# A windowed multi-level attention and a mixture of experts, one layer in float32: weights laid out by the host, biases carried by the last weight row

## The chip, the cores and the metric

The kernel runs on one core of a Trainium2 chip. The metric is the device time of one execution in microseconds; the time before is the median of three runs. The whole program is written by hand against five engines: TensorE (PE, with its weight loads PEld), VectorE (DVE), ScalarE (ACT), GpSimd (POOL) and SyncE (SP), which here only issues DMAs.

## The reference

x has 2 x 1024 tokens of 128 channels. One layer: x = x + attention(layernorm(x)), then x = x + experts(layernorm(x)).

```python
qkv = x @ W_attn + b_attn                  # 128 -> 384, 16 heads of 8 channels
q, k, v = split(qkv, 3)
# level 0: each query sees the 64 keys up to its own; levels 1 to 4: the 8 mean-pooled keys
# of the previous block of 64, 128, 256, 512 tokens (pools of 8, 16, 32, 64 tokens)
mn = min over levels of max(A_level)       # the shift of the exponentials
out = sum over levels of scale * exp(A - mn) / esum @ (v, pooled v)
x = x + out @ W_proj + b_proj
...
gate = softmax(x @ Wg.T); keep the best 2 of 8, divide by their sum
for e in range(8):                         # all experts are computed, and weighted
    a, b = split(x @ W1[e].T + b1[e], 2)   # 128 -> 2 x 256
    out += ((a * sigmoid(b)) @ Wo.T + bo) * comb[..., e]
```

## The kernel before

A function schedule() writes one list of steps, and every engine runs through that one list and does its own part of each step. So each engine's order is fixed by hand, and the engines are tied by semaphores. An instruction that waits holds up all that stands behind it on its engine.

Precision: a product of two float32 tensors is made of three products of fast-format (fp32r) parts, high x high, high x low, low x high (`split3`, L1045 to L1047). For that each operand is split: a copy writes the high part, a subtraction the low part. A few products are plain float32, which the profile counts as two instructions each.

Attention. Batch b goes in four units of 4 heads, units 0 to 3 for batch 0 and 4 to 7 for batch 1. Before a batch's units: `stat` and `apply` (layer norm, xnorm), `xT` (four PE transposes, xT_hi copied by ScalarE, xT_lo by VectorE), `pool` (pooled means of xT, 128 x 512: xpool_hi, xpool_lo), `qk` (query and key products, q, k times 512 tokens each), `kp` (pooled keys), `v` and `pv` (values and pooled values, four groups each). In a unit, tiles of `score` are followed three tiles later by their `out` products (L1198, L1199), with ScalarE's exponential and VectorE's `mask` (L978) in between. `guard` (VectorE maxima of pooled scores, L954 to L957), `shift` and `shiftT` give the shift row of the next unit. SP moves the parts of q, k and pooled k of a unit's heads into the tiles qst, kst and pks by DMA; `heads` (`head_columns`, L410, or L408 on VectorE) spreads pks into pkm, one column set per head.

Where biases are handled before:
- q, k: `bias` makes columns of the q and k bias (two products of one row, L1061) and of b1 (a transpose, L1062); VectorE copies both (L886, L887). ScalarE and VectorE add the column while they split q and k (L685, L928).
- pooled k: VectorE adds the column and multiplies with a mask of real blocks (L934), then copies the high part (L936) and subtracts (L937).
- v, pooled v: in each of the four groups of a step a fourth product of 2 rows adds the bias, split into two rows (L1087, L1093). `constants` (L830 to L835) makes these rows on VectorE. There are two v steps and one pv step in each batch.
- w1: a channel of ones is put in the last column of xnorm (L722), the last column of w1 is taken from the others by GpSimd (L622), and b1 put in its place (L623). Layer-normed channels sum to zero, so that one of them can be given up.

Weights: `weights` permutes and scales W_attn on VectorE (L819 to L823) and splits it (L824, L825). W1 comes as it is, (expert, 512, 128), in tiles of 256 KB, through a ring of STAGES = 4 buffers; the steps `w1` stand at score tiles 1, 1, 2, 3, 4, 6, 7 and 9 of the last unit: SP's load, GpSimd's subtraction (L622, L623), four PE transposes (L1122), ScalarE's copy of the high part (L701) and VectorE's subtraction (L1001). `w2` does the same for Wo and Wg (L1126, L1127). One of three general banks of PSUM is used by each step of the set GENERAL in turn.

Experts (from about 222 us): for each of 16 tiles of 128 tokens and each of 8 experts three products of 512 columns, a sigmoid, a product with the gate on VectorE (L1028), an addition on GpSimd (L654), then two transposes and the output product.

The first instructions of GpSimd are memsets: of qmk (128 x 4096), vwin and vaug (128 x 2048, and four narrow ones, L607), for each of two buffers.

## Time and profile before

| what | us |
|---|---|
| median of 3 runs | 335.55 |
| all three runs | 335.55, 331.0, 336.18 |
| the profiled execution, its time | 336.18 |
| its span, first to last instruction | 336.2 |
| TensorE busy | 305.9 (91%) |
| VectorE busy | 226.8 (67%) |
| ScalarE busy | 178.1 (53%) |
| GpSimd busy | 142.3 (42%) |
| mean granted TensorE clock | 0.929 |

The profile shows one execution. Busy is the time in which an engine has an instruction in flight, so for TensorE, whose instructions overlap, a busy stretch need not be a fast one. The clock that was granted to TensorE is given as a share of 2.4 GHz, so 0.5 is 1.2 GHz. HBM read is 4.21 MB and written 1.05 MB over the span.

### The profile page before, as it was taken

The page shows a single profiled execution, that of the slowest core. Times are in us where ns is not written, and L with a number is a line of the kernel's source. Part 1 is how long each engine was busy: PE and PEld are TensorE (multiplying, and loading weights), DVE is VectorE, ACT ScalarE, POOL GpSimd, SP SyncE. Part 2 cuts the span into 40 slices and gives each one's busy share as a digit, 9 for nine tenths or more (in the row PEclk, how much of TensorE's full clock was granted, in tenths as well). Part 3 has the DMA queues.
Part 4 walks back from the last instruction along what each step waited for, and adds up shares of the span by engine and source line. Part 5 has one row for each costly group of instructions (what it writes and reads, how often), then busy time and mean ns, then how long its engine had stood idle before and what let it go on. Part 6 is the DMA issues. An engine that isn't in the chain of part 4 may idle for free.

```text
span 336.2 us, 6934 instructions
## 1 busy us (share of the span) xinstructions
PE 305.9 (91%) x2384; PEld 260.7 (78%) x2384; DVE 226.8 (67%) x660; ACT 178.1 (53%) x366; POOL 142.3 (42%) x232
## 2 busy tenths in 40 slices
PE   0268699899999999999999999999999999999995
PEld 0246589788988989887989899886888867888884
DVE  6997408987585550285666655947786798777773
ACT  1513166557546842654576654574548655555552
POOL 3990011330012100010050665208778847888882
PEclk9997555999999997589999979999999999999999
DMA  7005405252304500033526013000000000000000
GB/s 225 27 1 121 104 18 117 57 118 59 96 11 94 127 18 10 1 89 101 118 64 179 11 50 108 4 10 8 8 10 18 11 0 16 11 16 8 11 17 17
DMA packets 15881, 17.51 MB, mean 52 GB/s; under 512 B 2235, under 2 KB 12646, under 8 KB 15846
## 3 DMA queue, kind: packets, MB, share of 16 engines
q1 hardware_dynamic: 15648, 16.85, 19.4%
q8 instruction: 19, 0.31, 0.4%
q10 hardware_dynamic: 198, 0.22, 0.3%
q14 instruction: 16, 0.13, 0.1%
HBM read 4.21 MB, written 1.05 MB: 16 GB/s over the span
## 4 chain that ended last, share of the span: by engine, by line
PE 76%; DVE 14%; issue 4%; ACT 3%; POOL 1%; DMA 1%; ACTq 0%; DVEq 0%
PE bank L1198 16%; PE bank L1045 12%; PE bank L1047 11%; PE bank L1046 11%; PE bank L1172 5%; PE bank L1179 4%; PE bank L1199 4%; PE bank L1100 2%; PE bank L1159 2%; PE bank L1087 2%; DVE xnorm L802 2%; DVE lmax L954 2%; PE bank L1122 2%; DVE work L978 1%; DMA xres<-L_attn_x 1%
## 5 line engine op out<-in xcount | busy, mean ns | idle before, releaser
L654 POOL TENSOR_TENSOR work<-work 128x256 f32<-128x256 f32 x110 | 80.9, 739 | 33.6 <-DVE work L1028 21.0
L1198 PE MATMUL bank<-work,vaug 128*64 128x64 f32 x1024 | 84.1, 231 | 0.3 <-issue 0.3
L1198 PEld LDWEIGHTS bank<-work,vaug 128*64 128x64 f32 x1024 | 72.8, 143 | 8.9 <-issue 1.2
L1028 DVE SCALAR_TENSOR_TENSOR work<-bank,comb,work 128x256 f32<-128x256 f32 x128 | 59.1, 480 | 25.7 <-ACT work L759 24.4
L759 ACT ACTIVATE work<-bank 128x256 f32<-128x256 f32 x128 | 48.4, 385 | 44.7 <-PE bank L1047 44.5
L978 DVE TENSOR_TENSOR work<-work,const 128x512 f32<-128x512 f32 x64 | 46.2, 734 | 18.0 <-ACT work L737 17.4
L586 POOL COPY vaug<-vwin 128x64 f32<-128x64 f32 x64 | 16.1, 298 | 94.8 <-ACT vwin L697 48.0
L737 ACT ACTIVATE work<-bank 128x512 f32<-128x512 f32 x64 | 37.5, 594 | 27.2 <-PE bank L1179 26.8
L1199 PE MATMUL bank<-work,vpool 128*64 128x64 f32 x256 | 36.9, 227 | 0.0
L562 POOL TENSOR_TENSOR rstd<-veps,nhalf 128x4 f32<-128x4 f32 x8 | 11.5, 1432 | 49.6 <-DVE veps L794 49.5
L1179 PE MATMUL bank<-qmk,kst 98*128 98x256 f32 x128 | 31.0, 328 | 0.0
L1045 PE MATMUL bank<-qmk,xT_hi 128*128 128x512 f32 x64 | 27.4, 428 | 0.1
L1045 PE MATMUL bank<-qmk,kst 128*128 128x512 f32 x64 | 26.5, 414 | 0.0
L1199 PEld LDWEIGHTS bank<-work,vpool 128*64 128x64 f32 x256 | 26.2, 143 | 0.0
L1047 PE MATMUL bank<-qmk,xT_lo 128*128 128x512 f32 x64 | 25.3, 395 | 0.0
L1046 PE MATMUL bank<-arena,xT_hi 128*128 128x512 f32 x64 | 25.3, 395 | 0.0
L1047 PE MATMUL bank<-qmk,kst 128*128 128x512 f32 x64 | 25.1, 392 | 0.0
L1046 PE MATMUL bank<-arena,kst 128*128 128x512 f32 x64 | 25.0, 391 | 0.0
L410 ACT ACTIVATE pkm<-pks,const 96x512 fp32r<-96x512 f32 x30 | 20.8, 712 | 5.5 <-DMA pks<-kpool_hi 5.5
L1179 PEld LDWEIGHTS bank<-qmk,kst 98*128 98x128 f32 x128 | 21.6, 209 | 2.4 <-issue 0.8
L954 DVE TENSOR_REDUCE lmax<-bank 128x12 f32<-128x96 f32 x64 | 13.5, 252 | 13.1 <-PE bank L1100 12.6
L1172 PE MATMUL bank<-qst,pkm 104*128 104x64 f32 x128 | 20.0, 309 | 0.0
(194 smaller groups left out, 534.6 us busy)
## 6 DMA issues: line engine op xcount, KB each, us to landing
qst<-arena SPq DMA_DIRECT2D x24, 128.0 KB, 2.3
kst<-arena SPq DMA_DIRECT2D x24, 128.0 KB, 2.3
qmk<-qst SPq DMA_DIRECT2D x32, 96.0 KB
pks<-kpool_hi SPq DMA_DIRECT2D x16, 64.0 KB, 2.0
xnorm<-L_ffn_W SPq DMA_DIRECT2D x4, 256.0 KB, 2.9
out<-yout SPq DMA_DIRECT2D x16, 64.0 KB, 1.5
xres<-L_attn_x SPq DMA_DIRECT2D x2, 256.0 KB, 4.2
xres<-L_attn_x SPq DMA_DIRECT2D x1, 512.0 KB, 7.3
```

The source lines that it names most:

```text
L654: gp.tensor_tensor(gacc[t % 2][:, :], gacc[t % 2][:, :], gtmp[(adds - 1) % TMP_RING][:, :], ALU.add).then_inc(acc_done, 1)
L737: act.activation(prob[lo % P_RING][:, :, :, :], bank[sc % SCORE_BANKS][:, :].rearrange("p (c j q) -> p c j q", c=2, j=GH), ACT.Exp).then_i ...
L759: act.activation(sig[hn % SIG_RING][:, :], bank[hn % HID_BANKS][:, HID:2 * HID], ACT.Sigmoid).then_inc(sig_done, 1)
L978: dve.tensor_tensor(prob[lo % P_RING][:, :, :, :].rearrange("p c j q -> p (c j) q"), prob[lo % P_RING][:, :, :, :].rearrange("p c j q -> p ...
L1028: dve.scalar_tensor_tensor(dst[:, :], bank[hn % HID_BANKS][:, 0:HID], comb[:, t, e:e + 1], sig[hn % SIG_RING][:, :], ALU.mult, ALU.mult).t ...
L1045: pe.matmul(out, lhs[0], rhs[0], start=start, stop=False)
L1046: pe.matmul(out, lhs[0], rhs[1], start=False, stop=False)
L1047: return pe.matmul(out, lhs[1], rhs[0], start=False, stop=stop)
L1172: ins = pe.matmul(out[:, k * WIN:(k + 1) * WIN], pkm[s][0:SR + 2 * GH, c, :, :].rearrange("p j k -> p (j k)"), qst[s][0:SR + 2 * GH, c * W ...
L1179: ins = pe.matmul(out[:, k * 256:(k + 1) * 256], kst[s][0:SR + 2, c * WIN:c * WIN + P], qmk[s][0:SR + 2, :, c * WIN:(c + 1) * WIN], start= ...
L1198: pe.matmul(o, vaug[hu % 2][:, c % 8, j, :], prob[lo % P_RING][:, i, j, :], start=(j == 0), stop=False)
L1199: ins = pe.matmul(o, vpool[:, c, u % NG, :], probp[u % 2][:, c, :], start=False, stop=True)
```

## The change

The host now hands over weights that are already laid out. W_attn comes with q and k columns permuted, W1 transposed to (128, 8, 512), Wo and Wg transposed. For wqkv, w1 and wg it comes in two planes: in plane 0 the last row is the bias, in plane 1 every row holds a copy of the last row of the weights, its own last row being zero. Plane 0 minus plane 1 is then the weight with its last row taken from all others and the bias in its place. The last channel of xnorm is one, for the first layer norm too, and GpSimd writes these ones once (`ones_ready`). So the sums over 128 rows bring the bias with them:

- gone: the step `bias` (three TensorE instructions, two VectorE copies), the four copies and scalings of `weights` and bias_perm, the step `constants`, the 24 bias products, the 32 transposes of w1, the three of wo and wg, the four ScalarE copies of ones, GpSimd's column copies of w1 and its two steps on wg, and three small loads on ScalarE's queue;
- pooled k: padded blocks of xpool are zero in all rows, so no mask. ScalarE makes the high part from PSUM, VectorE the low part;
- q is scaled while it is split (0.35 or 1 as a number, no bias column);
- w1: GpSimd subtracts plane 1 from plane 0 (128 x 512), ScalarE copies the high part from SBUF, VectorE subtracts from SBUF. Tiles are of 512 KB, the ring has 3 buffers, two of them new. The first two loads wait for nothing new, the third for the second x2T step, and each later one for VectorE's subtraction of the tile three before (`w1_ready`);
- wqkv is one load of 384 KB; the constants shrink from 504 KB to 182 KB.

```diff
-GENERAL = {"bias", "xT", "qk", "kp", "v", "pv", "guard", "shiftT", "spread", "proj", "w1", "w2", "x2T", "gatelog", "hidT", "y"}
+GENERAL = {"xT", "qk", "kp", "v", "pv", "guard", "shiftT", "spread", "proj", "x2T", "gatelog", "hidT", "y"}
-ACT_FIRST = {"xT", "qk", "w1", "x2T"}
+ACT_FIRST = {"xT", "qk", "kp", "x2T"}
...
-    s += [("qk", 0, 0, 0), ("qk", 0, 0, 1), ("kp", 0), ("constants",), ("qk", 0, 1, 0), ("qk", 0, 1, 1)]
+    s += [("qk", 0, 0, 0), ("qk", 0, 0, 1), ("kp", 0), ("qk", 0, 1, 0), ("qk", 0, 1, 1)]
...
-STAGES = 4
+STAGES = 3
...
+    def paired(w, bias):
+        rows = np.array(w, np.float32)
+        rows[C - 1] = bias
+        last = np.array(np.broadcast_to(w[C - 1], w.shape), np.float32)
+        last[C - 1] = 0.0
+        return rows, last
...
             def load_w1(n):
-                sp.dma_start(w1_stage[n % STAGES], w1_d[n].rearrange("(t p) c -> p t c", p=P)).then_inc(w1_in[n % STAGES], 16)
+                sp.dma_start(w1_stage[n % STAGES][:, :, :], w1_d[:, n]).then_inc(w1_in[n % STAGES], 16)
...
                 if u + 2 == UNITS:
-                    wait_gen_full(sp, ("pv", 1))
-                    wait_gen_full(sp, ("x2T", 0, 0))
                     for i in range(STAGES - 1):
                         load_w1(i)
             wait_gen_full(sp, ("x2T", 0, 1))
             load_w1(STAGES - 1)
             for n in range(STAGES, E):
-                wait_gen_done(sp, ("w1", n - STAGES))
+                sp.wait_ge(w1_ready, n - STAGES + 1)
                 load_w1(n)
...
+            gp.memset(xnorm[:, :, C - 1:C], 1.0).then_inc(ones_ready, 1)
             blank_keys(0)
             rstd_of(0)
...
-            def fix_w1(n):
+            def whole_w1(n):
                 st = w1_stage[n % STAGES]
-                wait_gen_done(gp, ("bias",))
                 gp.wait_ge(w1_in[n % STAGES], 16 * (n // STAGES + 1))
-                then(gp.tensor_tensor(st[:, :, 0:C - 1], st[:, :, 0:C - 1], st[:, :, C - 1:C].broadcast_to([P, 4, C - 1]), ALU.subtract))
-                gp.tensor_copy(st[:, :, C - 1:C], b1_col[:, 4 * n:4 * n + 4].unsqueeze(2)).then_inc(w1_fixed, 1)
+                gp.tensor_tensor(st[:, 0, :], st[:, 0, :], st[:, 1, :], ALU.subtract).then_inc(w1_whole, 1)
...
-                elif step == ("gatelog", 0, 1):
-                    for n in range(STAGES):
-                        fix_w1(n)
-                elif step[0] == "w1" and step[1] >= STAGES:
-                    fix_w1(step[1])
+                elif step[0] == "w1":
+                    whole_w1(step[1])
...
+                elif kind == "kp":
+                    b = step[1]
+                    wait_gen_full(act, step)
+                    if b:
+                        act.wait_ge(pks_in, 48 * NG)
+                    act.activation(kpool_hi[:, :], gen_bank(step)[:, :], ACT.Copy).then_inc(gen_hi, 1)
...
                 elif kind == "w1":
                     n = step[1]
-                    wait_gen_full(act, step)
-                    act.activation(w1T_hi[:, n, :], gen_bank(step)[:, :], ACT.Copy).then_inc(gen_hi, 1)
+                    act.wait_ge(w1_whole, n + 1)
+                    act.activation(w1T_hi[:, n, :], w1_stage[n % STAGES][:, 0, :], ACT.Copy).then_inc(w1_high, 1)
...
-                    ins = dve.tensor_scalar(xnorm[:, t, :], xres[:, t, :], mv[:, o + i, 0:1], rstd[:, o + i:o + i + 1], ALU.subtract, ALU.mult)
+                    ins = dve.tensor_scalar(xnorm[:, t, 0:C - 1], xres[:, t, 0:C - 1], mv[:, o + i, 0:1], rstd[:, o + i:o + i + 1], ALU.subtract, ALU.mult)
...
-                dve.wait_ge(wattn_in, 64)
-                dve.tensor_scalar(by_row(bias_perm[:, 0:C]), by_d(bias_row[:, 0:C]), QSCALE, None, ALU.mult)
-                dve.tensor_copy(by_row(bias_perm[:, C:2 * C]), by_d(bias_row[:, C:2 * C]))
-                dve.tensor_scalar(by_row(wqkv[:, 0:C]), by_d(wattn[:, 0:C]), QSCALE, None, ALU.mult)
-                dve.tensor_copy(by_row(wqkv[:, C:2 * C]), by_d(wattn[:, C:2 * C]))
-                then(dve.tensor_copy(wqkv[:, 2 * C:3 * C], wattn[:, 2 * C:3 * C]))
+                dve.wait_ge(wqkv_in, 16)
+                then(dve.tensor_tensor(wqkv[:, 0, :], wqkv[:, 0, :], wqkv[:, 1, :], ALU.subtract))
...
-                    then(dve.scalar_tensor_tensor(kpool[:, :], bk[:, :], bias_col[:, 1:2], const[:, C_PADMASK:C_PADMASK + NB * LK],
-                                                  ALU.add, ALU.mult))
-                    then(dve.tensor_copy(kpool_hi[:, :], kpool[:, :]))
-                    dve.tensor_tensor(kpool_lo[:, :], kpool[:, :], kpool_hi[:, :].bitcast(F32), ALU.subtract).then_inc(gen_dve, 1)
+                    dve.tensor_tensor(kpool_lo[:, :], bk[:, :], kpool_hi[:, :].bitcast(F32), ALU.subtract).then_inc(gen_dve, 1)
...
-                    pe.wait_ge(cst_ready, 1)
                     pe.wait_ge(xt_ready, 2 * b + n + 1)
...
-                        split3(out, (xT_hi[:, rows], xT_lo[:, rows]), wv, stop=False)
-                        ins = pe.matmul(out, rows2[:, NB * LK:NB * LK + P], bv2[:, :], start=False, stop=True)
+                        ins = split3(out, (xT_hi[:, rows], xT_lo[:, rows]), wv)
...
-                    for i in range(4):
-                        ins = pe.transpose(bk[:, i * P:(i + 1) * P], w1_stage[step[1] % STAGES][:, i, :], ident)
```

What moves on the engines is shown at three places, before first and then now; the names are tiles, written <- read.

VectorE at the start, from the end of the layer norm of batch 0 on. Before (attT holds the weights, denom the bias):

```order
L819 TENSOR_SCALAR attT<-denom 1x128
L820 COPY attT<-denom 1x128
L821 TENSOR_SCALAR attT<-attT 128x128
L822 COPY attT<-attT 128x128
L823 COPY attT<-attT 128x128
L824 CAST wqkv_hi<-attT 128x384
L825 TENSOR_TENSOR wqkv_lo<-attT,wqkv_hi 128x384
L905 TENSOR_TENSOR xT_lo<-bank,xT_hi 128x512
L906 TENSOR_REDUCE pool_sum<-bank 128x64
L905 TENSOR_TENSOR xT_lo<-bank,xT_hi 128x512
L906 TENSOR_REDUCE pool_sum<-bank 128x64
L886 COPY bias_col<-bank 128x2
```

Now, at the same place, with planes and result both in attT:

```order
L807 TENSOR_TENSOR attT<-attT 128x384
L808 CAST wqkv_hi<-attT 128x384
L809 TENSOR_TENSOR wqkv_lo<-attT,wqkv_hi 128x384
L873 TENSOR_TENSOR xT_lo<-bank,xT_hi 128x512
L874 TENSOR_REDUCE pool_sum<-bank 128x64
L873 TENSOR_TENSOR xT_lo<-bank,xT_hi 128x512
L874 TENSOR_REDUCE pool_sum<-bank 128x64
L881 TENSOR_TENSOR pool_sum<-pool_sum 128x64
```

Five small steps in front of the cast became one wider subtraction, and the copies behind the pooled sums are gone.

TensorE in the first v step of batch 1, behind the third unit's out products. Before:

```order
L1045 MATMUL bank<-wqkv_hi,xT_hi 128x128
L1046 MATMUL bank<-wqkv_lo,xT_hi 128x128
L1047 MATMUL bank<-wqkv_hi,xT_lo 128x128
L1087 MATMUL bank<-bv,rows 128x128
L1045 MATMUL bank<-wqkv_hi,xT_hi 128x128
L1046 MATMUL bank<-wqkv_lo,xT_hi 128x128
L1047 MATMUL bank<-wqkv_hi,xT_lo 128x128
L1087 MATMUL bank<-bv,rows 128x128
```

Now:

```order
L1012 MATMUL bank<-wqkv_hi,xT_hi 128x128
L1013 MATMUL bank<-wqkv_lo,xT_hi 128x128
L1014 MATMUL bank<-wqkv_hi,xT_lo 128x128
L1012 MATMUL bank<-wqkv_hi,xT_hi 128x128
L1013 MATMUL bank<-wqkv_lo,xT_hi 128x128
L1014 MATMUL bank<-wqkv_hi,xT_lo 128x128
```

The fourth product of each group is gone; the groups follow each other directly.

SP's queue of loads at the last unit of attention, where xpool, kpool and xnorm served as buffers of w1. Before:

```order
L437 DMA xpool<-L_ffn_W 128x4x128 [waits gen_full]
L437 DMA kpool<-L_ffn_W 128x4x128
L437 DMA xnorm<-L_ffn_W 128x4x128
L434 DMA qmk<-nshiftT 2x32x128 [waits gen_dve]
L434 DMA qst<-nshiftT 8x8x128
L437 DMA xnorm<-L_ffn_W 128x4x128 [waits gen_full]
L437 DMA xpool<-L_ffn_W 128x4x128 [waits gen_dve]
L437 DMA kpool<-L_ffn_W 128x4x128 [waits gen_dve]
L437 DMA xnorm<-L_ffn_W 128x4x128 [waits gen_dve] x2
```

Now, with w_stage for the two new buffers:

```order
L441 DMA w_stage<-w 128x1024 x2
L438 DMA qmk<-nshiftT 2x32x128 [waits gen_dve]
L438 DMA qst<-nshiftT 8x8x128
L441 DMA xnorm<-w 128x1024 [waits gen_full]
L441 DMA w_stage<-w 128x1024 [waits w1_ready] x2
L441 DMA xnorm<-w 128x1024 [waits w1_ready]
L441 DMA w_stage<-w 128x1024 [waits w1_ready] x2
```

The first loads lost their wait, one fewer is made ahead, and the later ones wait for VectorE's subtraction of w1 (`w1_ready`).

## Rows read from the trace of the kernel before

**Rows 1.** Busy time by stretch: stretch, length, PE, PEld, DVE, ACT, POOL, PEclk, DMA, GB/s

```profile
3.00:4.00 1.00, 0.00 (x0) 0.00 (x0) 0.62 (x2) 0.75 (x1) 0.00 (x0) 1.00 1.11 338
30.20:57.50 27.30, 24.43 (x100) 20.90 (x100) 12.64 (x50) 13.40 (x26) 2.49 (x9) 0.50 0.33 80
125.80:129.20 3.40, 3.40 (x33) 3.28 (x31) 0.22 (x1) 2.07 (x4) 0.00 (x0) 0.51 0.07 19
132.60:146.30 13.70, 13.70 (x70) 12.42 (x69) 5.10 (x15) 8.97 (x19) 1.48 (x8) 0.50 0.02 4
206.00:222.00 16.00, 16.00 (x209) 14.71 (x207) 12.76 (x52) 7.87 (x15) 5.38 (x10) 1.00 0.07 20
222.00:336.00 114.00, 109.90 (x544) 88.94 (x542) 82.86 (x227) 62.07 (x162) 83.73 (x116) 1.00 0.04 11
```

**Rows 2.** Timeline of the start, VectorE and GpSimd: start us, us, engine, line, operation

```profile
14.61 1.09 POOL L607 MEMSET vaug<- 128x64 f32 x4
...
15.40 0.51 DVE L824 CAST wqkv_hi<-attT 128x384 fp32r<-128x384 f32 x1
...
15.94 0.56 DVE L825 TENSOR_TENSOR wqkv_lo<-attT,wqkv_hi 128x384 fp32r<-128x384 f32 x1
...
20.68 1.80 POOL L605 MEMSET vaug<- 128x2048 f32 x1
20.71 2.06 DVE L922 CAST xpool_hi<-xpool 128x512 fp32r<-128x512 f32 x1
...
22.55 0.54 POOL L607 MEMSET vaug<- 128x64 f32 x4
```

**Rows 3.** Timeline, pooled keys, key splits and head columns of units 0 and 1

```profile
25.30 0.75 DVE L934 SCALAR_TENSOR_TENSOR kpool<-bank,bias_col,const 128x512 f32<-128x512 f32 x1 [0.48 <-PE bank L1047]
...
26.08 0.43 DVE L936 CAST kpool_hi<-kpool 128x512 fp32r<-128x512 f32 x1
...
26.54 0.69 DVE L937 TENSOR_TENSOR kpool_lo<-kpool,kpool_hi 128x512 fp32r<-128x512 f32 x1
...
28.76 1.39 DVE L928 SCALAR_TENSOR_TENSOR arena<-bank,bias_col,arena 128x512 fp32r<-128x512 f32 x2
...
30.45 1.33 ACT L410 ACTIVATE pkm<-pks,const 96x512 fp32r<-96x512 f32 x2 [2.34 <-DMA pks<-kpool_hi]
...
45.04 2.55 ACT L410 ACTIVATE pkm<-pks,const 96x512 fp32r<-96x512 f32 x4
```

**Rows 4.** Timeline of TensorE, v products around a bias product, at both clocks

```profile
122.04 0.27 PE L1046 MATMUL bank<-wqkv_lo,xT_hi 128*128 128x128 f32 x1
122.15 0.27 PE L1047 MATMUL bank<-wqkv_hi,xT_lo 128*128 128x128 f32 x1
...
122.61 0.33 PE L1045 MATMUL bank<-wqkv_hi,xT_hi 128*128 128x128 f32 x1
...
138.49 0.41 PE L1047 MATMUL bank<-wqkv_hi,xT_lo 128*128 128x128 f32 x1
...
139.24 0.48 PE L1045 MATMUL bank<-wqkv_hi,xT_hi 128*128 128x128 f32 x1
```

**Rows 5.** Timeline of the last unit of attention, w1 beside it

```profile
200.09 0.37 SPq L437 DMA_DIRECT2D xpool<-L_ffn_W  x1
...
201.61 0.66 PE L1122 MATMUL bank<-const,xnorm 128*128 128x128 f32 x4
...
202.03 0.48 PE L1179 MATMUL bank<-qmk,kst 98*128 98x256 f32 x2
...
203.14 1.03 POOL L622 TENSOR_TENSOR xpool<-xpool 128x508 f32<-128x508 f32 x1 [4.28 <-DMA xpool<-L_ffn_W]
...
203.55 1.18 DVE L978 TENSOR_TENSOR work<-work,const 128x512 f32<-128x512 f32 x1
...
205.13 0.60 ACT L701 ACTIVATE qmk<-bank 128x512 fp32r<-128x512 f32 x1 [1.74 <-PE bank L1122]
```

**Rows 6.** DMA issues of w1 tiles: KB each, median us from issue to landing

```profile
xnorm<-L_ffn_W SPq DMA_DIRECT2D x4, 256.0 KB, 2.9
```

More of the change, by code:

```diff
@@ L136, in schedule @@
 def schedule():
-    s = [("stat", 0, 0), ("stat", 0, 1), ("apply", 0, 0), ("apply", 0, 1), ("weights",), ("xT", 0, 0), ("xT", 0, 1), ("bias",), ("pool", 0)]
-    s += [("qk", 0, 0, 0), ("qk", 0, 0, 1), ("kp", 0), ("constants",), ("qk", 0, 1, 0), ("qk", 0, 1, 1)]
+    s = [("stat", 0, 0), ("stat", 0, 1), ("apply", 0, 0), ("apply", 0, 1), ("weights",), ("xT", 0, 0), ("xT", 0, 1), ("pool", 0)]
+    s += [("qk", 0, 0, 0), ("qk", 0, 0, 1), ("kp", 0), ("qk", 0, 1, 0), ("qk", 0, 1, 1)]
     s += [*[("heads", 0, j) for j in range(GH)], ("weight columns",), ("v", 0, 0), *[("guard", 0, m) for m in range(4)], ("shift", 0), ("shiftT", 0)]
@@ L163, in schedule @@
         5: {5: [("stat2", 0, 0)], 8: [("apply2", 0, 0)]},
-        6: {0: [("x2T", 0, 0)], 4: [("stat2", 0, 1)], 7: [("apply2", 0, 1)], 8: [("w2",), ("x2T", 0, 1)]},
+        6: {0: [("x2T", 0, 0)], 4: [("stat2", 0, 1)], 7: [("apply2", 0, 1)], 8: [("gate weights",), ("x2T", 0, 1)]},
         7: {0: [("gatelog", 0, 0)], 3: [("gatelog", 0, 1)], 4: [("gatelog", 0, 2)], 5: [("gatelog", 0, 3)],
@@ L342, in build @@
         zero_ready = sem("zero_ready")
+        ones_ready = sem("ones_ready")
         heads_ready = sem("heads_ready")
@@ L1057, in _ @@
                         wait_gen_done(pe, GEN[n - GEN_BANKS])
-                if kind == "bias":
-                    pe.wait_ge(wqkv_ready, 1)
-                    for t in range(2):
-                        ins = pe.matmul(bk[:, t:t + 1], bias_perm[0:1, t * C:(t + 1) * C], const[0:1, C_ONES:C_ONES + 1], start=True, stop=True)
-                    ins = pe.transpose(bk[:, P:P + 4 * E], b1_rows, ident[0:4 * E, 0:4 * E])
-                elif kind == "xT":
+                if kind == "xT":
                     _, b, n = step
```

168 lines of the change are left out of this document (60 added, 108 removed).

## The prediction

> **What bounds the kernel now.** I read the table of stretches first. From 222 us on, the expert phase, TensorE is busy 109.90 of 114.00 us at the full clock [rows 1]; the change edits nothing that repeats there, so a third of the span is fixed. In the attention before it TensorE is the late engine too, but its clock falls to half for three stretches: 30.2 to 57.5, 125.8 to 129.2 and 132.6 to 146.3, 44 us in all [rows 1]. In the first of them TensorE counts as busy 24.43 of 27.30 us while VectorE does 12.64; what it runs at the half clock is then paid double. Then the timeline of the start: up to 30 us VectorE carries the path and TensorE waits for it (xnorm, weights, xT_lo, pooling). Last the stretch from 206 to 222 us, where w1 is prepared beside the last unit of attention: TensorE 16.00 of 16.00 busy, VectorE 12.76 [rows 1]. So work taken from VectorE pays before 30 us, work taken from TensorE pays in 35 to 50 and 120 to 150 us, and at 206 to 222 us it pays only until VectorE is late.
>
> **The profiled execution.** It is the run of 336.18 us, its span 336.2; nothing lies around it. The median of the three runs is 335.55, the fastest 331.0. I sum against 336.2 and read the result against 335.55.
>
> **Start, VectorE up to the keys.** The four permuting copies (L820 to L823) stand beside GpSimd's four small memsets at 14.61, and the cast behind them begins at 15.40 [rows 2]: 0.8 us, 0.2 each. They give way to one subtraction of 128x384, for which I take the 0.56 of L825, the same size [rows 2]: 0.2 saved. The two copies of bias columns (L886, L887) go, which wait for nothing by then; by the permuting copies they are worth 0.4, but they are narrower, and I take 0.2. Then comes a race. The cast of xpool_hi took 2.06 us, its twin of kpool_hi 0.43 [rows 2, 3]: it was issued at 20.71, 0.03 us behind a GpSimd memset of 1.80 us, and ended when that ended. 0.4 us earlier it would be in front. But the four small memsets took 1.09 us beside the permuting copies and 0.54 without them [rows 2], so GpSimd comes 0.5 us earlier too and again stands in front by about 0.1. I take the cast as still blocked and ending with the memset, 0.75 us earlier in all; the other end is 2.2 us, if it slips ahead. The new subtraction reads two SBUF tensors and the memsets read none. The Trainium skill (SBUF — State Buffer, Who interferes with whom) says that a copy or cast takes the port pair shared with GpSimd while a subtraction of two SBUF tensors meets only GpSimd instructions that read; the trace agrees for the copies (1.09 against 0.54), and shows no such subtraction.
> Pooled keys: behind the products three VectorE steps ran from 25.30 to 27.23 [rows 3]. Now ScalarE copies (0.60, as L701 in rows 5) and VectorE subtracts (0.69): about 1.4, so 0.55 saved. Their DMAs, issued by SP behind it, and the first head columns (ScalarE, 30.45 [rows 3]) come 1.3 us earlier. The split of the v bias, six small steps between 27.23 and 28.76 [rows 3], leaves VectorE; TensorE's v products waited for it, and ScalarE's v copies, which free the bank of the third guard, waited for them. I put another 1.3 us on this, 2.6 in all when the first shift row is transposed. Against it: wqkv comes as 384 KB instead of 192 beside the first x tile; at 338 GB/s [rows 1] half of the extra 192 KB is 0.3 us, taken off.
>
> **The 24 bias products on TensorE.** From the product before one to the product behind it: 0.46 us at the full clock (122.15 to 122.61), 0.75 at half (138.49 to 139.24) [rows 4]. Without it that step lies between the 0.11 inside a group (122.04 to 122.15 [rows 4]), which would make the bias product worth 0.35, and half of the 0.46, which makes it 0.23; I take 0.27, and at the half clock 0.48 (up to 0.53). Of six groups of four, the first ran while others waited; the second and the pooled one of batch 0 lie in the slow stretch, 1.9 us each. From the second group on, ScalarE waits for its DMA of pooled keys instead, so I count 0.7 of it until the head columns of unit 1 (45.04 [rows 3]) and 1.8 for the pooled one. The start gives 2.6 + 0.7 + 1.8 - 0.3 = **4.8 us**, bounds 2.5 and 7. Batch 1: two groups at full clock, 1.1 each, one at half, 1.9: **4.1 us**, TensorE having no idle time there.
>
> **The clock in batch 1.** Both falls, at 125.8 and 132.6 [rows 1], come right behind a group of v or pooled v products, the first of which is the group of 122.04 [rows 4]. In such a group four products of 2 rows stand among twelve full ones; without them it is 1.1 us shorter, and the dense out products beside it move up. If the two falls vanish, 3.4 + 1.2 us of out products run at twice the speed (2.3 us), and score, v and key products up to 146.3 gain 1 to 2 us more, ScalarE's head and pool copies then being late (8.97 us busy of 13.70 [rows 1]). Bounds 0 and 4.3; I take **3.0**.
>
> **The end of attention.** Eight groups of four transposes of w1 go, 0.42 us each (201.61 to 202.03 [rows 5]): 3.4; three products of wo and wg, 0.4 by the same row. But w1 now comes in three stages of 512 KB where it had four of 256 KB. The reload is triggered as before, when the first stage is free (SP, 200.09 [rows 5]), but brings tile 3, where it brought tile 4. Landing: 2.9 us for 256 KB [rows 6] and 0.8 for the rest at 338 GB/s, an estimate of 3.7. Then GpSimd subtracts 128x512 with two full inputs, 1.0 to 1.4 (1.03 [rows 5]), and ScalarE copies at 200.09 + 3.7 + 1.3 = 205.1. It copied tile 3 at 205.13 [rows 5]. So the time freed in front of it is absorbed by this wait: behind it in ScalarE's queue stand the exponentials of the next score tiles, which TensorE needs three tiles later, so it is not held, but VectorE's queue (subtraction, mask, gates) starts no earlier. From 206 on VectorE has 3.2 us idle [rows 1], which bounds the gain; half a microsecond of it lies behind its last gate step, and eight subtractions that now read two SBUF tensors meet GpSimd's reading (a mask took 1.18 beside GpSimd's of 203.14 [rows 5], where 128x512 is else worth the 0.69 of L937 [rows 3]), some 0.5 lost. **2.3 us**, and 0.6 for gate and wo; 0 to 4.4. The same section of the Trainium skill has that contention as its rule, two SBUF inputs against GpSimd reads; the mask agrees.
> ScalarE loses four column copies, VectorE's xnorm a column, both hidden by TensorE: nothing. The rest is the same.
> Sum: 4.8 + 4.1 + 3.0 + 2.9 = 14.8, so 336.2 - 14.8 = **321.4 us**.
>
> **Rivals.** A: the clock falls in batch 1 as before. For it: score tiles and v products remain sparse around 134 us. 324.4, and with the end worth less, up to 327. B: the cast wins its race, the keys come 1.4 us earlier and the rest goes by the upper bounds: 313 to 317. C: the w1 ring becomes the path. Two rounds of reload must fit between 200.09 [rows 5] and about 219 us; each is the landing plus 1.3 on GpSimd, 0.6 on ScalarE and 0.7 on VectorE. It decides when a landing takes over some 6 us, (18.9 - 5.2) / 2 = 6.8 with none of the queues in between busy; at 9 us two rounds cost 5 more and the gain at the end turns into a loss: 326 to 329. D, slower: the clock stays at half after the start. TensorE now has longer holes around 30 us, waiting for keys and shifts, and the attention behind them at half clock pays 0.5 us for each us so spent. It must outlast the present 57.5 us by 24 us to eat the 11.8 us of the other terms, by 38 to be 2% slower: about 343 to 350. Against it: the out products that stand at 57.5 come earlier and are unchanged. E: all is hidden, at 331 to 335: the start would have to wait for a DMA that no row shows as late.
>
> **Chances.** Forecast (318 to 324) 0.45, A 0.24, B 0.13, C 0.11, D 0.02, E 0.05. Eight in ten lie between 315 and 328.5. Within 2% of 335.55, about what a measurement of this kernel can tell from no change, means over 328.8: the top of C and all of E, 0.1.
>
> **What would show it.** The first head columns near 29.2 us, those of unit 1 near 41.7 (30.45 and 45.04 [rows 3]); xpool_hi again about as long as a memset or 0.4 us (B). No half clock at 125 to 132 less the 5 us gained (A: it is there). ScalarE waiting for GpSimd before the copy of w1 tile 3, one wait of 2 to 3 us; waits before tiles 5 to 7 as well would be C. First expert product some 14.8 us before the 222 us of [rows 1]. The forecast is wrong if the start gives under 3 us, or if half-clock time grows.

## The result, and the profile after

The changed kernel takes 323.06 us (median of four runs, 322.82 to 323.71), the kernel before 335.87 (four runs, 331.0 to 336.33): a ratio of 0.970, 95% interval 0.962 to 0.978. The forecast was 321.4. The changed kernel ran twice more, on two chips, at 323.58 and 323.30 us. Nearly all its executions lie between 322.6 and 324.6; those of the kernel before, over all chips, between 330.7 and 339.4. The ratios here and below leave out executions that lie more than 1.5% above the fastest of their kernel, so they differ a little from the quotients of the medians.

First a correction of the base. The profiled execution of the changed kernel took 322.97 us and spans 320.8. Executions of the kernel before that were listed with both numbers took 1.8 us more than their span, 337.92 for 336.1 in one. So the one with the span of 336.2 took about 338.0 and was not the run of 336.18: it stood 2 us above the median. Span against span the change gives 15.4 us, where the sum was 14.8. Median against median it gives 12.8.

The profile's page of the changed kernel, busy time by engine and the granted clock in 40 slices:

```profile
span 320.8 us, 6751 instructions
PE 285.0 (89%) x2320; PEld 244.2 (76%) x2320; DVE 221.3 (69%) x643; ACT 178.1 (56%) x364; POOL 142.6 (44%) x223
PEclk9999557999999999699999979999999999999999
```

Busy time by stretch, to be held against [rows 1]; the first three are the stretches at half clock, the fourth is the last unit of attention, the last the experts:

```profile
31.80:52.20 20.40, 15.96 (x80) 14.96 (x80) 10.36 (x46) 11.05 (x23) 2.49 (x9) 0.51 0.33 82
127.20:134.20 7.00, 5.96 (x34) 5.26 (x34) 3.83 (x12) 5.40 (x10) 1.99 (x8) 0.52 0.16 36
185.40:188.90 3.50, 3.50 (x28) 3.09 (x27) 2.03 (x4) 3.02 (x6) 0.00 (x0) 0.56 0.56 156
181.22:206.40 25.18, 23.73 (x279) 21.76 (x277) 17.97 (x60) 13.79 (x25) 10.69 (x10) 0.93 0.37 124
206.40:320.80 114.40, 110.10 (x544) 88.94 (x542) 82.97 (x227) 62.00 (x160) 83.83 (x116) 1.00 0.04 11
```

The experts are as they were (114.4 against 114.0 us, PE 110.10 against 109.90). The half clock at the start lasts 20.4 us where it lasted 27.3 (23.9 in e10, the changed kernel once more). Of the two falls around 130 us one is left, 7.0 us in place of 17.1. The third row, at 185 us, is not new: the kernel before has the same short fall in its last unit, which [rows 1] and the prediction's "three stretches" leave out. It is in both kernels and explains none of the gain; in the kernel before it is

```profile
197.40:200.80 3.40, 3.40 (x21) 3.18 (x21) 1.27 (x2) 2.38 (x5) 1.37 (x3) 0.50 0.02 5
```

The timeline of the start, to be held against [rows 2, 3]:

```profile
12.93 1.81 POOL L608 MEMSET vaug<- 128x2048 f32 x1
13.16 1.66 DVE L807 TENSOR_TENSOR attT<-attT 128x384 f32<-128x384 f32 x1
...
16.62 3.52 POOL L598 MEMSET qmk<- 128x4096 f32 x1
...
19.13 1.05 DVE L885 TENSOR_SCALAR xpool<-pool_sum 128x120 f32<-128x120 f32 x4
...
20.19 1.81 POOL L608 MEMSET vaug<- 128x2048 f32 x1
...
20.22 2.06 DVE L890 CAST xpool_hi<-xpool 128x512 fp32r<-128x512 f32 x1
...
24.81 0.60 ACT L681 ACTIVATE kpool_hi<-bank 128x512 fp32r<-128x512 f32 x1 [4.52 <-PE bank L1014]
...
29.44 1.33 ACT L414 ACTIVATE pkm<-pks,const 96x512 fp32r<-96x512 f32 x2 [1.48 <-DMA pks<-kpool_hi]
```

The cast was issued half a microsecond earlier, and so was the memset: it stands 0.03 us behind it again and takes 2.06 us again. These rows show that it was no race. The last of the four scalings of xpool in front of the cast waits for the memset of qmk (it ends at 20.14, the scalings at 20.18), and GpSimd's next memset begins right behind that end. In the kernel before the two ends are 20.63 and 20.67, in e5 below the lag is 0.03 us again (20.47 and 20.49). So here GpSimd's memsets set the pace in both kernels, and 0.4 us less work on VectorE could not have put the cast in front. The new subtraction ends with a memset too: 1.66 us in place of the 0.56 taken for it. The step ahead of it was held as long, so this cost nothing: the cast of wqkv_hi begins 0.53 us earlier (14.87 for 15.40). The first head columns start at 29.44 us (29.2 was forecast), those of unit 1 at 41.31 (41.7).

The timeline of the last unit, w1 tile 3 on its way through SP, GpSimd, ScalarE and VectorE, to be held against [rows 5]:

```profile
185.87 0.93 SPq L441 DMA_DIRECT2D w_stage<-w  x2
...
189.86 2.50 POOL L624 TENSOR_TENSOR w_stage<-w_stage 128x512 f32<-128x512 f32 x2 [5.09 <-DMA w_stage<-w]
...
191.16 0.63 ACT L696 ACTIVATE qmk<-w_stage 128x512 fp32r<-128x512 f32 x1 [2.65 <-POOL w_stage L624]
...
191.82 1.09 DVE L968 TENSOR_TENSOR arena<-w_stage,qmk 128x512 fp32r<-128x512 f32 x1 [2.14 <-ACT qmk L696]
```

From the load at 185.87 to GpSimd's first subtraction pass 3.99 us (3.7 had been estimated for the landing), ScalarE waits 2.65 us for it and VectorE 2.14 us for ScalarE. That is the wait that the prediction put there. Before, TensorE was busy for all 27.03 us of this unit; now for 23.73 of 25.18.

Where the time went is best seen at fixed points of the program. The table has when each begins, in us of the span, for every kernel of this study (the experiments follow below):

| kernel | first out product | v, batch 1 | unit 4 | unit 5 | unit 7 | experts | span |
|---|---|---|---|---|---|---|---|
| before | 55.31 | 121.87 | 133.83 | 159.24 | 195.01 | 222.04 | 336.2 |
| changed | 49.99 | 116.57 | 123.44 | 145.53 | 181.22 | 206.40 | 320.8 |
| e0_after_again | 49.95 | 116.51 | 123.38 | 145.46 | 181.14 | 206.14 | 320.5 |
| e10_after_third | 50.04 | 116.62 | 123.48 | 145.63 | 181.30 | 206.43 | 320.8 |
| e1_products_back | 53.05 | 119.63 | 132.18 | 157.69 | 193.36 | 219.92 | 334.3 |
| e2_products_second_half | 50.21 | 116.80 | 127.20 | 152.62 | 188.31 | 213.25 | 327.6 |
| e3_before_without_products | 51.30 | 117.87 | 124.73 | 146.84 | 182.60 | 209.54 | 323.7 |
| e9_full_row_products | 50.80 | 117.39 | 125.14 | 153.10 | 189.18 | 214.76 | 329.1 |
| e11_before_full_rows | 52.12 | 118.69 | 126.45 | 148.56 | 184.32 | 211.33 | 325.5 |
| e4_four_stages | 50.04 | 116.60 | 123.47 | 146.07 | 181.74 | 205.12 | 319.5 |
| e12_two_stages | 50.04 | 116.62 | 123.49 | 145.59 | 181.27 | 214.81 | 329.3 |
| e5_memset_in_eighths | 48.84 | 115.40 | 122.26 | 144.88 | 180.55 | 206.40 | 320.7 |
| e7_all_memsets_in_eighths | 44.35 | 110.92 | 117.79 | 139.88 | 175.56 | 200.49 | 314.8 |
| e8_stages_and_eighths | 44.18 | 110.77 | 117.64 | 139.74 | 175.42 | 199.28 | 313.6 |

So the 15.4 us come from the start (5.3 at the first out product), from 121 to 159 us (another 8.4), and from the last unit (1.85); nothing from anywhere else, and the experts take 0.2 us more. From the first out product to v of batch 1 every kernel takes 66.6 us.

### The profile page after: what moved, and what is told of

Read it like the earlier page. It is cut to its first block, busy times and chain, and to the rows that moved or that the text cites. A ratio compares the mean times of both kernels' runs of the same rounds, so it can differ in the third digit from the quotient of the medians.

```text
span 320.8 us, 6751 instructions
## 1 busy us (share of the span) xinstructions
PE 285.0 (89%) x2320; PEld 244.2 (76%) x2320; DVE 221.3 (69%) x643; ACT 178.1 (56%) x364; POOL 142.6 (44%) x223
## 3 DMA queue, kind: packets, MB, share of 16 engines
HBM read 6.16 MB, written 1.05 MB: 22 GB/s over the span
## 4 chain that ended last, share of the span: by engine, by line
PE 65%; DVE 19%; ACT 5%; DMA 4%; issue 4%; POOL 2%; SPq 1%; DVEq 0%; ACTq 0%
PE bank L1148 14%; PE bank L1012 11%; PE bank L1014 10%; PE bank L1013 10%; PE bank L1122 4%; PE bank L1129 4%; DVE work L940 3%; PE bank L1149 3%; PE bank L1060 3%; PE bank L1109 2%; DVE xnorm L796 2%; DVE lmax L916 2%; ACT vpool L400 1%; DMA xres<-x 1%; PE bank L1068 1%
## 5 line engine op out<-in xcount | busy, mean ns | idle before, releaser
L1148 PEld LDWEIGHTS bank<-work,vaug 128*64 128x64 f32 x1024 | 72.1, 142 | 10.3 <-DVE work L940 1.8
L588 POOL COPY vaug<-vwin 128x64 f32<-128x64 f32 x64 | 18.5, 336 | 79.1 <-PE bank L1149 43.4
L1122 PE MATMUL bank<-qst,pkm 104*128 104x64 f32 x128 | 18.1, 291 | 1.4 <-DMA qst<-nshiftT 1.4
```

What stands on the lines that cost most here:

```text
L1122: ins = pe.matmul(out[:, k * WIN:(k + 1) * WIN], pkm[s][0:SR + 2 * GH, c, :, :].rearrange("p j k -> p (j k)"), qst[s][0:SR + 2 * GH, c * W ...
L1148: pe.matmul(o, vaug[hu % 2][:, c % 8, j, :], prob[lo % P_RING][:, i, j, :], start=(j == 0), stop=False)
```

## Experiments on the bias products

All are run beside the kernel before, on the same chip; the changed kernel is repeated with e1, e2 and e3 (as e0) and with e8 and e9 (as e10), the other runs were made without it on their chips. The profiled executions of e1 and e9 were longer than the median of their kernel (336.12 against 334.68, 330.9 against 325.51), that of e7 shorter (316.97 against 319.33); what is said of their totals goes by the medians.

**e0_after_again**, no edit.

> The changed kernel unedited, on the chip of the runs sent with it, as their base. Expected: 322.5 to 324 us, half clock again in three stretches (about 20, 7 and 3.5 us long).

323.58 us (322.62 to 326.07), half clock from about 31, 126.5 and 184.5 us.

**e1_products_back**, and the same for pooled v; zrow holds zeros.

```diff
-                        ins = split3(out, (xT_hi[:, rows], xT_lo[:, rows]), wv)
+                        ins = split3(out, (xT_hi[:, rows], xT_lo[:, rows]), wv, stop=False)
+                        ins = pe.matmul(out, zrow[:, :], wqkv_hi[0:2, 2 * C:3 * C], start=False, stop=True)
```

> The changed kernel with a fourth product of 2 rows (all zeros) put back behind each of the 24 groups of three of v and pooled v; it adds nothing to the sums. Theory (the prediction's): the products cost 2.5 us in batch 0 (0.7 and 1.8) and 4.1 in batch 1, and with them the clock falls at 125.8 and 132.6 come back, 3.0: 332 to 333 us in all, with a half-clock stretch right behind the first v group of batch 1. Rival 1, the products alone: the falls stay away, 329 to 330. Rival 2, the products were hidden in the kernel before: under 326.

334.68 us (329.04 to 338.02; ratio to the kernel before 0.990, 0.982 to 0.998), over the 332 to 333 that were expected. By the medians 11.1 us of the gain are gone again by this edit alone; the host's layout and all that left VectorE, ScalarE and GpSimd is still in it. But its ten executions differ by 9 us, and the granted clock says why. Span times 2 times (1 - mean clock) gives the time at half clock: 31 us in the two shortest (spans of 327.2 and 327.4, mean clock 0.953), as many as in two of e0 (320.5 and 322.1, both 0.952); 46 us in one of 331.3 (0.931), 55 in the profiled one of 334.3 (0.918). So the products cost 5 to 7 us with no more half clock than in the changed kernel, and what the longer ones lost beyond that goes with more half clock. (Where the mean clock is above 0.96 this sum can't be used: the record can lack a stretch, see e3.) Its timeline of TensorE in the first v group of batch 1, and its busy time in two stretches at half clock:

```profile
121.37 0.28 PE L1016 MATMUL bank<-wqkv_hi,xT_lo 128*128 128x128 f32 x1
121.58 0.32 PE L1052 MATMUL bank<-wqkv_hi,zrow 2*128 2x128 f32 x1
121.83 0.33 PE L1014 MATMUL bank<-wqkv_hi,xT_hi 128*128 128x128 f32 x1
```

```profile
122.60:126.40 3.80, 3.80 (x38) 3.59 (x38) 0.88 (x2) 2.95 (x5) 0.00 (x0) 0.55 0.06 17
129.60:146.90 17.30, 17.30 (x91) 15.66 (x92) 7.30 (x20) 9.13 (x20) 1.47 (x8) 0.51 0.12 27
```

From the product before that of 2 rows to the one behind it are again 0.46 us, as in [rows 4], and both falls of the clock are back in this execution, the first right behind the v group, which runs from 119.63 to about 122.6.

**e2_products_second_half**: the same edit, for batch 1 alone.

```diff
-                        ins = split3(out, (xT_hi[:, rows], xT_lo[:, rows]), wv)
+                        ins = split3(out, (xT_hi[:, rows], xT_lo[:, rows]), wv, stop=not b)
+                        if b:
+                            ins = pe.matmul(out, zrow[:, :], wqkv_hi[0:2, 2 * C:3 * C], start=False, stop=True)
```

> As the run with all products back, but the product of 2 zero rows stands only behind the 12 groups of batch 1. Theory: 4.1 us of products and up to 3.0 of clock, 329 to 330.5 us; the start up to the first out product as in the changed kernel (50.0 us). Rival, the clock falls of the kernel before were tied to what batch 0 did before them, not to the products beside them: 327 us, no half clock at the v group of batch 1.

329.60 us (328.80 to 330.86), 6.0 over the changed kernel. At unit 5 it is 7.2 us behind e0 and 0.3 of that stood there at the first out product. One long stretch at half clock, by the busy time in it:

```profile
125.80:140.00 14.20, 14.20 (x79) 12.92 (x77) 5.43 (x17) 9.09 (x19) 1.48 (x8) 0.52 0.02 6
```

In e0 it is 6.8 us long there. The rival's 327 us is out. But it was right that no fall comes with the v group in this run (it ended near 120); the one fall there is comes half a microsecond behind the pooled v group (its last product begins at 125.11). In the changed kernel the fall at 127 comes 5 us behind that group, so "right behind the group" does not hold as a rule.

**e3_before_without_products**: the kernel before, without L1087 and L1093 (the v bias is left out).

```diff
-                        split3(out, (xT_hi[:, rows], xT_lo[:, rows]), wv, stop=False)
-                        ins = pe.matmul(out, rows2[:, NB * LK:NB * LK + P], bv2[:, :], start=False, stop=True)
+                        ins = split3(out, (xT_hi[:, rows], xT_lo[:, rows]), wv)
```

> The kernel before without its 24 products of 2 rows (the v bias is left out of the result), all else as it was. Theory: 2.5 us of batch 0, 4.1 of batch 1 and 3.0 of clock are the products' share, so 9.6 us under the kernel before, near 326 us, and no half clock at 125.8 and 132.6 less the gain ahead of them. Rival, the falls are owed to the score tiles around them, and the products to nothing but their own time: 329 to 330, with half clock near 130 for about 17 us as before.

325.60 us (324.23 to 325.73; ratio 0.973, 0.963 to 0.984): four fifths of the whole gain with none of the change's other parts (10.3 of 12.3 us by the medians of this chip, 12.5 of 15.4 by spans). The time is as expected; that no half clock would be left at this place is not: the stretch around 130 us is 7.2 us long, as in the changed kernel:

```profile
28.80:56.00 27.20, 22.42 (x110) 20.72 (x111) 16.36 (x60) 14.57 (x28) 2.49 (x9) 1.00 0.42 101
127.70:134.90 7.20, 6.21 (x38) 5.50 (x38) 3.58 (x12) 6.17 (x12) 1.99 (x8) 0.53 0.12 29
```

The first of these rows nearly misled me: the clock record says 1.00 from 28.8 to 56 us, as if the fall at the start were gone. The timeline of the same stretch says otherwise:

```profile
30.41 0.41 PE L1046 MATMUL bank<-wqkv_lo,xT_hi 128*128 128x128 f32 x1
30.62 0.41 PE L1047 MATMUL bank<-wqkv_hi,xT_lo 128*128 128x128 f32 x1
```

The step is 0.21 us, twice the 0.11 of the full clock [rows 4], and the steps stay that long until about 56 us. The record was missing, not the half clock.

**e9_full_row_products**: as e1, with

```diff
-        zrow = sb("zrow", [2, P], F32R)
+        zrow = sb("zrow", [P, P], F32R)
-                        ins = pe.matmul(out, zrow[:, :], wqkv_hi[0:2, 2 * C:3 * C], start=False, stop=True)
+                        ins = pe.matmul(out, zrow[:, :], wqkv_hi[:, 2 * C:3 * C], start=False, stop=True)
```

> As the run with the 24 products back, but each takes 128 rows of zeros in place of 2. It has the same columns and the same count. Theory (what the products of 2 rows cost is their own shape: the step over one took 0.35 us more at full clock where a product of 128 rows takes 0.11): each costs 0.11 us, 0.21 at half clock, 4 us in all, and the clock goes as in the changed kernel: 325 to 328 us. Rival: any fourth product costs what those of 2 rows did and brings the longer half clock: 333 to 335.

325.51 us (324.57 to 330.90; ratio 0.976, 0.969 to 0.984): 2.2 us over the changed kernel on its chip (e10), where e1, with the same number of products and columns, was 11.1 over it on its own (e0). The timeline of TensorE, first v group of batch 1:

```profile
118.56 0.28 PE L1016 MATMUL bank<-wqkv_hi,xT_lo 128*128 128x128 f32 x1
118.67 0.28 PE L1052 MATMUL bank<-wqkv_hi,zrow 128*128 128x128 f32 x1
118.78 0.27 PE L1014 MATMUL bank<-wqkv_hi,xT_hi 128*128 128x128 f32 x1
```

0.11 us for the product of 128 rows. A group of three takes 0.33 us, with a product of 128 zero rows 0.44, with one of 2 rows 0.74 (121.09 to 121.83 in e1). So a product of 2 rows costs 0.40 us at full clock and one of 128 costs 0.11. In the profiled execution, the longest at 330.9 us, there is no half clock from 121 to 136 us but some from 140 to 154: the clock can still fall, and the medians have to say how often that matters.

The Trainium skill (TensorEngine Tiling (Array Packing), Key Properties) says that TensorE is drained when the tiling mode changes. These rows fit that: in e1 the steps are 0.21 us ahead of the product of 2 rows, 0.25 behind it and 0.16 behind the next, where 0.11 is usual. The change from products of 128 columns to the out products of 64 shows it too: 0.20 us from 121.93 to 122.13 in the changed kernel, where 0.11 is usual. That the product of 2 rows ran in another mode, no row says; from the last product of 104 rows to the next of 128 rows it is 0.11 us (163.64 to 163.75 in the changed kernel).

**e11_before_full_rows**: the same on the kernel before; `constants` fills all rows of rows2 and the first two of bv2.

```diff
-        rows2 = sb("rows2", [2, NB * LK + P], F32R)
-        bv2 = sb("bv2", [2, C], F32R)
+        rows2 = sb("rows2", [P, NB * LK + P], F32R)
+        bv2 = sb("bv2", [P, C], F32R)
...
+            dve.memset(bv2[:, :].bitcast(F32), 0.0)
```

> The kernel before, with its weights, transposes and constants as they were; its 24 bias products now have 128 rows, of which 126 are zeros, and give the same sums. Theory (two rows are what was dear): the run without these products was 12.5 us shorter in its profile and 24 products of 128 rows cost 2.7 us at full clock and up to 1.2 more at half, so 326 to 329 us where the kernel before takes 332 to 336 on the same chip. Rival: in the kernel before, the products' place counts and not their rows, and it stays within 2 us of the kernel before.

327.30 us (325.95 to 327.84) against 336.42 on that chip (ratio 0.972, 0.969 to 0.974): 9.1 us less. By spans it is 10.7 of the change's 15.4, seven tenths, had by padding an operand with zeros. (Ratios of different chips are not compared here, since the kernel before had medians from 332.0 to 336.4.) The time at half clock around 130 us is down to

```profile
132.60:136.00 3.40, 3.40 (x25) 3.18 (x26) 2.66 (x9) 3.06 (x6) 1.31 (x5) 0.50 0.08 19
```

## Experiments on the ring of w1 and on the start

**e4_four_stages**: a fourth buffer, where the pooled keys lie (kpool_hi and kpool_lo become the halves of kpool_parts); for that the first loads wait until the last pooled keys have been moved (`pks_in`).

```diff
-STAGES = 3
+STAGES = 4
-            ... sb("w1_stage2", [P, 2, 2 * HID]), xnorm[:, 0:TT, :].rearrange("p (n t) c -> p n (t c)", n=2)]
+            ... sb("w1_stage2", [P, 2, 2 * HID]), kpool_parts[:, :, :].bitcast(F32), xnorm[:, 0:TT, :].rearrange("p (n t) c -> p n (t c)", n=2)]
```

> The changed kernel with four stages for w1 instead of three (the fourth lies where the pooled keys were), so that tile 3 is loaded before the last unit. Theory (the reload absorbs part of what the transposes gave back): ScalarE's 2.65 us wait at 191.16 and VectorE's 2.14 us wait behind it go, the first expert product comes 1 to 2 us earlier, 321.3 to 322.3 us. Rival: VectorE has as many instructions before the first expert product as it has time, and waits somewhere else: under 0.5 us, 323.

321.72 us (321.34 to 323.67; ratio 0.968, 0.951 to 0.985, a wide interval since the kernel before spread on that chip); 1.3 to 1.9 us under the changed kernel's three medians. The last unit takes 23.38 us in place of 25.18. Part of this can be the clock: this profile has no half clock in the last unit, the changed kernel's has 3.4 us of it. e7 and e8 below, both with a short fall there, give 24.93 us with three buffers and 23.86 with four, 1.1 us. ScalarE, timeline of the last unit:

```profile
188.92 0.62 ACT L697 ACTIVATE qmk<-xnorm 128x512 fp32r<-128x512 f32 x1
...
191.57 0.63 ACT L697 ACTIVATE qmk<-w_stage 128x512 fp32r<-128x512 f32 x1 [1.55 <-POOL w_stage L625]
```

Tile 3 no longer waits; tile 4 now does, 1.55 us where tile 3 waited 2.65.

**e12_two_stages**; `w1_stage2` leaves the list of buffers.

```diff
-STAGES = 3
+STAGES = 2
```

> The changed kernel with two stages for w1 in place of three. Theory (the ring is on the path in the last unit, and each reload of a stage takes the DMA and three engines, 5 to 7 us): only two tiles are ready ahead and six are loaded behind one another in pairs, three rounds in place of two, so the last unit gets 3 to 6 us longer, 326 to 329 us. Rival: the last unit is held by VectorE's own work, and the ring costs under 1 us, 324.

330.88 us (330.34 to 331.46; ratio 0.983, 0.980 to 0.985). The sign is right and the size is not: 7.3 to 7.8 us over the changed kernel's three medians, more than the upper end of 6. Timeline of ScalarE in the last unit:

```profile
191.05 0.63 ACT L696 ACTIVATE qmk<-w_stage 128x512 fp32r<-128x512 f32 x1 [3.77 <-POOL w_stage L624]
...
197.90 0.63 ACT L696 ACTIVATE qmk<-w_stage 128x512 fp32r<-128x512 f32 x1 [4.43 <-POOL w_stage L624]
...
210.47 0.63 ACT L696 ACTIVATE qmk<-xnorm 128x512 fp32r<-128x512 f32 x1 [3.45 <-POOL xnorm L624]
```

Besides the three waits, the granted clock in this profile is at half from 195 to 205.5 and from 212 to 215.5 us, which neither theory had; how much of the loss it took was not separated. The last unit takes 33.5, 25.2 and 23.4 us with two, three and four stages.

**e5_memset_in_eighths**

```diff
-                then(gp.memset(vaug[i][:, :, :, :], 0.0))
+                for k in range(NB // 2):
+                    ins = gp.memset(vaug[i][:, k, :, :], 0.0)
+                then(ins)
```

> The changed kernel with GpSimd's two memsets of vaug (1.81 us each) written as eight of an eighth. Theory: the cast of xpool_hi is held by the one memset it meets, so it takes at most 0.7 us in place of 2.06, and pooled keys, first head columns and all behind them come 1.3 to 1.4 us earlier: 321.7 us. Rival: GpSimd keeps the cast waiting through all eight in a row, 2 us again, and the time stays at 323.

323.06 us (321.95 to 325.00). The cast that was meant is freed, and the time doesn't follow. The cast of xpool_hi, which meets the first of the eight pieces (they run from 20.47 to 22.83), and TensorE late in the last unit:

```profile
20.49 0.56 DVE L892 CAST xpool_hi<-xpool 128x512 fp32r<-128x512 f32 x1
```

```profile
200.94 0.68 PE L1150 MATMUL bank<-work,vaug 128*64 128x64 f32 x8 [2.10 <-DVE work L942]
```

The first out product comes 1.15 us earlier than in the changed kernel, unit 7 still 0.7, the experts not at all. Half a microsecond is lost between unit 4 and unit 5, beside the stretch at half clock, as in e4, where no instruction up to there is another than in the changed kernel. The rest goes in the last unit, at w1: GpSimd waits 5.13 and then another 0.98 us for the two tiles loaded together (one of these loads took 5.5 us to land, in the changed kernel none there over 4.8), ScalarE 2.63 and 1.40 us for GpSimd, TensorE up to 2.10 us for VectorE.

The pieces also did harm once, in an earlier place. The cast of wqkv_hi, 0.54 us in the changed kernel, was issued behind the third of the first eight pieces and ended 0.2 us behind the last of them (15.04):

```profile
12.88 2.16 POOL L609 MEMSET vaug<- 128x256 f32 x8
...
13.69 1.57 DVE L810 CAST wqkv_hi<-attT 128x384 fp32r<-128x384 f32 x1
```

That is what the rival had, VectorE kept waiting through a row of pieces, at a cast that the expectation did not look at.

**e7_all_memsets_in_eighths**: as e5, and

```diff
-                gp.memset(qmk[i][:, :, :].bitcast(F32), 0.0).then_inc(zero_ready, 1)
+                for j in range(8):
+                    ins = gp.memset(qmk[i][:, j // 2, (j % 2) * T // 2:(j % 2 + 1) * T // 2].bitcast(F32), 0.0)
+                ins.then_inc(zero_ready, 1)
```

> As the run with the vaug memsets in eighths, and the two memsets of qmk (3.51 us each) in eighths as well. In the changed kernel one of VectorE's eight xnorm steps, 0.33 us each without company, took 3.51. Theory, as above: each VectorE step waits for one piece of 0.45 us at most; xnorm takes 3 to 6 us in place of 6.91, and the start is 1 to 4 us shorter on top of the other 1.4: 317.5 to 321 us. Rival: every one of the eight steps now meets a piece, the sum is as before or longer: 322 to 324.

319.33 us (316.97 to 320.39; ratio 0.960, 0.945 to 0.976). VectorE's eight xnorm steps and GpSimd's eight pieces beside them:

```profile
7.93 2.45 DVE L800 TENSOR_SCALAR xnorm<-xres,mv,rstd 128x127 f32<-128x127 f32 x8
```

```profile
9.10 4.29 POOL L599 MEMSET qmk<- 128x512 f32 x8
```

In the changed kernel these xnorm steps took 6.91 us, one of them 3.51, as long as the memset (3.51). Now VectorE takes 0.31 us for each. Only the second four of them meet pieces: 1.21 us for the four (9.18 to 10.39), where the first four took 1.11. GpSimd's memset takes 4.29 us in all, 3.78 where it meets nobody (the second one, at 17.77). So here the loser of a meeting waits for one short instruction of the other. The Trainium skill (SBUF — State Buffer, Who interferes with whom) has the shared ports go to whoever issues first, for its whole instruction. The whole memset of 3.51 us with a VectorE step of 3.51 beside it agrees, and so do these steps; the cast of wqkv_hi in e5 does not, since five of the pieces that it waited for began after it had been issued. The first out product comes 5.6 us earlier than in the changed kernel, and the span is 6.0 us shorter in the profile (the shortest of the four executions), 3.7 to 4.3 by the medians. In this profile all that was gained is still there at the experts (5.9 us), with three buffers for w1.

**e8_stages_and_eighths**: e4 and e7 together, the best version of this study.

> The changed kernel with four stages for w1 and all four large memsets of GpSimd in eighths. Theory: the two lie in different stages of the program and add up: 5.6 us less until the first out product, 1.3 to 1.8 less in the last unit, 316 to 317.5 us, and less only by what the half clock in the middle varies. Rival: the earlier start only moves work into a longer half-clock stretch, 318.5 or more.

316.15 us (315.64 to 317.39), a ratio of 0.950 to the kernel before (0.944 to 0.955). On the same chip **e10_after_third**, the changed kernel once more, took 323.30 (322.75 to 324.59; ratio 0.972, 0.966 to 0.977): 7.15 us in favour of e8.

> The changed kernel unedited once more, as the base of the two runs sent with it: 322.5 to 323.7 us.

The start gives 5.9 us of it, and the last unit takes 23.86 us, 1.3 less. The rival is out: the half clock at the start lasts 23.9 us in e8 as in e10, and e8 still keeps all of the start's gain.

## The prediction, step by step

**The total** was right (321.4 for 323.06), and the sum of 14.8 stands against 15.4 by spans. Its base was wrong by 2 us: I took the profiled execution as the run of 336.18. With its own time of about 338.0 the sum would have given 323.2. That the sum came so close is partly luck: the middle gave 1.3 us more than its terms (8.4 for 7.1) and the end 1.05 less, and the products, priced too low, made up for a fall of the clock that stayed.

**The bias products** were mis-sized. I took 0.27 us each at full clock and 0.48 at half; measured 0.40 and, by the groups at half clock (1.24 us with, from 39.63 to 40.87 in the kernel before; 0.64 without, from 37.72 to 38.36 in e3), 0.60. Both lie above what I had called the upper end. The bound of 0.35 was one step less another; but the first step inside the next group is long too (0.16 us where 0.11 is usual), so whole groups had to be compared, not steps. With the clock, batch 1 gave 8.4 to 8.5 us where 4.1 and 3.0 stood; putting the products back costs 6.9 us there in e2's profile and 9.1 in e1's, which has more half clock.

**The clock** was right in part. One of the two falls around 130 us is gone, the other is shorter: 7.0 us in place of 17.1, where I had let all of it vanish. Rival A (both stay) is out, by the trace and by e1, which brings both back. Why a fall is left at 127 us was not tried. What the clock adds was not measured apart, but the lists of executions bound it. On e10's chip the three shortest of the kernel before have spans of 329.1 to 329.4 us at a mean clock of 0.948 (34 us at half clock), and two of the changed kernel 320.8 and 322.4 at 0.947, with as much of it: 7 to 8.5 us of the change come with equal time at half clock. The profiled execution of the kernel before, 336.2 at 0.929, had 48 us of it. So the other half of the 15.4 goes with 14 to 17 us more at half clock, and an execution of the kernel before that falls less has less to give back. The term of 3.0 was read off a long one. By the medians of e9 nearly all of both goes when the products have 128 rows (2.2 us are left of 11).

**The start** gave 5.3 us, 4.8 was forecast. Its split depends on the order of the edits. Taking the products away first (e3) gives 4.0 us, and the rest of the change 1.3. Doing the rest first (e1) gives 2.3 us, and the products 3.1. My 2.5 for the products and 2.3 for the rest is that second order with the products too small. The xpool_hi cast stayed blocked as said, but not by a lost race: its lag of 0.03 us is fixed by the memset of qmk in front, and the 0.49 us by which it moved are those by which GpSimd's memsets moved. Rival B, which let the race be won, could not have come about by this change; its price of the cast was about right (1.15 us in e5 for 1.4) and its total wrong: 313 to 317 where e5 gave 323.06. The 5.6 us of e7 lay in these memsets, which the prediction took as given.

**The end of attention** gave 1.85 us (27.03 to 25.18) where 2.3 and 0.6 stood. The wait before tile 3 came as described, at 2.65 us. Rival C was priced at 326 to 329 with three stages; its mechanism, the ring on the path, is there at a smaller size: a fourth stage takes 1.1 to 1.8 us off the unit. Whether the ring also takes up what is gained ahead of it is open: e5 lost 0.7 of its 1.15 us in this unit, with a slow landing, and e7 lost nothing.

**Rivals D and E** are out: the half clock at the start got shorter by 6.9 us (3.4 in e10), and nothing of the start was hidden behind a DMA.

## What to carry to other kernels

A matmul is not cheap because it has few rows: compare the time of a whole group with and without it, and try the same product with its operand padded to 128 rows of zeros before the work is moved elsewhere. A fix that shows no gain by itself (e5) can be part of one that does (e7, e8): look at the profile for where it was lost before you drop it. Where GpSimd clears large tiles beside VectorE's copies, casts or scalings, try clearing them in pieces, and look at every VectorE step that then meets them: most wait for one piece, one waited through the row (e5). And before a term is read off one execution, compare its mean granted clock with those of the others.

## What the runs showed of the hardware that I had not expected

- A product of 2 rows and 128 columns costs 0.40 us at full clock and 0.60 at half, one of 128 rows 0.11 and 0.21 (at full clock e1 and e9; at half clock the kernel before and e3).
- The record of the granted clock can lack a stretch: it says 1.00 in e3 from 28.8 to 56 us where the steps are those of 1.2 GHz. Of two executions of the kernel before on one chip, with spans of 334.6 and 334.3 us, the one lists a mean clock of 0.974 and the other 0.923. In the changed kernel too the record is 1.00 up to 28 us while a product of 512 columns takes 0.43 us from start to start (24.57 to 25.00); among the experts, at full clock, it takes 0.23 (206.97 to 207.20), and at 28.1 us the step of a product of 128 columns goes from 0.21 to 0.11. So that stretch was at 1.2 GHz. The Trainium skill (TensorE: Matmul & The Clock Gate, Back-to-back issue gap) gives the columns divided by 1.2 GHz as that step at the lower level, by which 512 columns take an estimated 427 ns, and warns under Seeing it yourself that the clock's events are not to be fully trusted; both agree. The step between equal products is the surer reading. The timeline of TensorE in the changed kernel, one such step at a record of 1.00:

```profile
24.57 0.63 PE L1012 MATMUL bank<-xT_hi,wqkv_hi 128*128 128x512 f32 x1
25.00 0.63 PE L1013 MATMUL bank<-xT_lo,wqkv_hi 128*128 128x512 f32 x1
```

- A memset of 3.51 us in eight pieces takes 3.78 alone and 4.29 beside VectorE; the four VectorE steps that met it took 1.21 us where four alone took 1.11 (e7). But a cast of 0.54 us beside smaller pieces took 1.57 (e5).
